# Second score pass eight slots behind the first, its rows of maxima sent by halves

## What is computed

```python
x = x + _L0_attn_ref(_layernorm(x, axis=-1), L0_attn_Wq, L0_attn_Wk, L0_attn_Wv, L0_attn_Wo)
x = x + _L0_xattn_ref(_layernorm(x, axis=-1), ctx_1024, L0_xattn_W_kv, L0_xattn_W_q, L0_xattn_W_proj, L0_xattn_b_proj)
x = x + _L0_ffn_ref(_layernorm(x, axis=-1), L0_ffn_gate_w, L0_ffn_w1, L0_ffn_b1, L0_ffn_w2, L0_ffn_b2)
```

## Time and profile before

| what | value |
|---|---|
| median of 3 runs | 202.76 us (201.15 to 203.41) |
| profiled execution | 200.95 us |
| its span, first to last instruction | 199.2 us |
| mean granted TensorE clock | 0.947 |
| TensorE busy | 166.8 us, 84% |
| VectorE busy | 140.7 us, 71% |
| ScalarE busy | 104.8 us, 53% |
| GpSimd busy | 52.3 us, 26% |

### The profile page before, as it was taken

The page is one execution under the profiler, slowest core; times in us unless marked ns, Lnnn a source line. Parts: engine busy times, 40 slices in busy tenths (PEclk is TensorE's granted clock), DMA queues, the critical chain, the costliest instruction groups (busy, mean ns, idle before and its releaser), DMA issues.

```text
span 199.2 us, 4411 instructions
## 1 busy us (share of the span) xinstructions
PE 166.8 (84%) x1500; PEld 116.1 (58%) x1508; DVE 140.7 (71%) x545; ACT 104.8 (53%) x222; POOL 52.3 (26%) x103
## 2 busy tenths in 40 slices
PE   0686195699599979989998998998998899799994
PEld 0343184485466755755764655654665556598984
DVE  2789299897347899799799889888968346525020
ACT  2132021257147656566566666766676657793451
POOL 7810005668800070030030030010115107126050
PEclk9999669589769999999999999999999999999999
DMA  5817660058227503322321321300340350170720
GB/s 150 238 35 175 164 173 18 3 148 184 70 82 196 184 25 104 110 69 58 109 82 49 98 95 35 90 0 3 113 130 3 100 143 0 17 224 26 229 66 26
DMA packets 23842, 19.05 MB, mean 96 GB/s; under 512 B 2364, under 2 KB 21820, under 8 KB 23100
## 3 DMA queue, kind: packets, MB, share of 16 engines
q1 hardware_dynamic: 22908, 17.79, 31.9%
q10 hardware_dynamic: 912, 0.98, 2.0%
HBM read 12.54 MB, written 2.49 MB: 75 GB/s over the span
## 4 chain that ended last, share of the span: by engine, by line
PE 50%; DVE 19%; DMA 15%; SPq 5%; issue 4%; POOL 3%; ACT 2%; POOLq 0%; DVEq 0%; ACTq 0%
PE psV L914 11%; PE psB L893 9%; PE psA L868 8%; DMA stackQ<-maxT 6%; DMA stackQ<-scratch 4%; DVE masked L623 4%; PE psA L958 4%; PE psM L923 3%; PE psA L975 3%; DMA stackK<-hid 3%; PE psV L975 3%; PE psM L933 3%; DVE stats L554 2%; DVE negmax L629 2%; SPq L402 2%
## 5 line engine op out<-in xcount | busy, mean ns | idle before, releaser
L753 ACT ACTIVATE E<-psB 128x512 f32<-128x512 f32 x112 | 62.3, 595 | 37.3 <-PE psB L893 15.7
L868 PE MATMUL psA<-stackK,stackQ 72*128 72x256 bf16 (+1 forms) x256 | 44.4, 277 | 11.8 <-DMA stackK<-hid 5.5
L893 PE MATMUL psB<-stackQ,stackK 74*128 74x256 bf16 (+1 forms) x256 | 42.2, 264 | 4.6 <-DMA stackQ<-maxT 3.8
L623 DVE CUSTOM_DVE_ANT_0 masked<-psA,row_mask 128x128 bf16<-128x128 f32 (+1 forms) x128 | 36.8, 352 | 11.8 <-PE psA L868 11.7
L629 DVE TENSOR_REDUCE negmax<-psA 128x2 f32<-128x512 f32 x64 | 39.7, 677 | 0.0
L868 PEld LDWEIGHTS psA<-stackK,stackQ 72*128 72x128 bf16 x256 | 23.0, 105 | 21.5 <-DMA stackQ<-scratch 8.6
L914 PE MATMUL psV<-E,V 128*9 128x256 f32 (+1 forms) x512 | 30.9, 359 | 0.2 <-ACT E L753 0.2
L893 PEld LDWEIGHTS psB<-stackQ,stackK 74*128 74x128 bf16 x256 | 22.0, 100 | 12.5 <-DMA stackQ<-maxT 5.6
L468 POOL TENSOR_SCALAR rstd<-mv 128x2 f32<-128x2 f32 x12 | 2.8, 236 | 89.1 <-DVE mv L558 88.9
L914 PEld LDWEIGHTS psV<-E,V 128*9 128x9 f32 x512 | 11.0, 90 | 14.4 <-issue 7.9
L761 ACT ACTIVATE oT<-psV 128x256 f32<-128x256 f32 x32 | 12.3, 384 | 7.9 <-PE psV L914 7.2
(11 more groups left out here) (111 smaller groups left out, 247.0 us busy)
## 6 DMA issues: line engine op xcount, KB each, us to landing
stackK<-scratch SPq DMA_DIRECT2D x18, 192.0 KB
stackQ<-hid SPq DMA_DIRECT2D x36, 64.0 KB
w1s<-w_dram SPq DMA_DIRECT2D x8, 258.0 KB, 2.8
w2s<-w_dram SPq DMA_DIRECT2D x8, 256.0 KB, 3.7
stackQ<-scratch SPq DMA_DIRECT2D x3, 576.0 KB
stackK<-hid SPq DMA_DIRECT2D x18, 64.0 KB
scratch<-hid SPq DMA_DIRECT2D x4, 192.0 KB, 3.7
scratch<-parts_ctx SPq DMA_DIRECT2D x4, 192.0 KB, 4.7
```

Of the source, the lines that this page charges most:

```text
L623: last = dve.tensor_tensor_reduce(out=masked[:, bank, i * keys:(i + 1) * keys], in0=scores[:, i, 0:keys], in1=row_mask[:, S - keys:S], sca ...
L753: act.activation(dst, psB[:, bank].rearrange("p (h q) -> p h q", h=dst.shape[1]), ACT.Exp, scale=SCALE).then_inc(b_taken, 1)
L868: last = pe.matmul(psA[:, bank, i * keys:(i + 1) * keys], stackQ[0:ROWS, b, h, t * P:(t + 1) * P], stackK[0:ROWS, b, h, 0:keys], start=Tru ...
L893: last = pe.matmul(psB[:, bank, i * n:(i + 1) * n], stackK[:, b, h, t * P:(t + 1) * P], stackQ[:, b, h, q0:S], start=(s == 1 or i == 0), s ...
```

## The change

- `LAG` is 8 instead of 11; `FFN_STEPS` puts `u0` to `u3` three slots nearer to `last`. All steps at LAG+10 and more after their job's first slot come three slots sooner; `stack_read_k` stays in its slot.
- The row of maxima goes in two halves of eight heads, each with its own transpose (`max_turn`, TensorE), copy to `maxT` and two DMAs (`max_rows`), in slots 4 and 8 after the job's first. In these slots `max_rows` stands ahead of the slot's units in the list, and `max_turn` behind them: VectorE does the copies before it takes the slot's maxima, TensorE transposes after the slot's scores. Only job 0 has both behind the units, in slot 8 also behind `rope` of batch 3. The second pass waits for the low half at group 0 and for the high half at group 2.
- Queries of cross-attention go to DRAM and back (`stack_put` at `q_cross`, `stack_get` two slots later) instead of by nine DMAs.
- `stack_write` and `stack_read` are cut into keys (1) and queries (0): batch 2's keys are written in slot 6, queries in 9, read in 9 and 10; batch 3's written in 13 and 14, read in 14 and 15 instead of 17.
- The projection of batch 3's queries and keys uses `psV` (`qk_bank`), and the memset of `psV` goes; the first `values` wait for the last rope instead. `masked` (a result that nobody reads) has two buffers instead of three.

```diff
-FFN_STEPS = ((-11, "u0"), (-10, "u1"), (-9, "u2"), (-8, "u3"), (-4, "u4"), (-3, "u5"), (-2, "u6"), (-1, "u7"),
+FFN_STEPS = ((-8, "u0"), (-7, "u1"), (-6, "u2"), (-5, "u3"), (-4, "u4"), (-3, "u5"), (-2, "u6"), (-1, "u7"),
              (1, "g0 g1"), (2, "d0 g2 d1"), (3, "d2 g3"), (4, "g4 g5 d3 d4"), (5, "s0 g6 g7 d5"), (6, "u8 d6"),
              (8, "d7 u9 d8"), (9, "s1 u10 d9 u11 d10 d11 s2"),
              (10, "u12 u13 d12 u14 d13 u15 d14 d15 s3"))
-LAG = 11
+LAG = 8
-    put(7, "max_rows", 0, 0)
...
-    put(9, "stack_write", 0, 2)
-    put(10, "stack_read", 0, 2)
-    put(14, "stack_write", 0, 3)
+    put(6, "stack_write", 0, 2, 1)
+    put(9, "stack_write", 0, 2, 0)
+    put(9, "stack_read", 0, 2, 1)
+    put(10, "stack_read", 0, 2, 0)
+    put(13, "stack_write", 0, 3, 1)
+    put(14, "stack_write", 0, 3, 0)
+    put(14, "stack_read", 0, 3, 1)
+    put(15, "stack_read", 0, 3, 0)
...
-        if j > 0:
-            put(n + 2 * NG, "max_rows", s, b)
-        if j == 1:
-            put(n + 2 * NG + 1, "stack_read", 0, 3)
+        for half in range(2):
+            if j == 0:
+                put(NG * (half + 1), "max_turn", 0, 0, half)
+                put(NG * (half + 1), "max_rows", 0, 0, half)
+            else:
+                row_of[n + NG * (half + 1)] = (s, b, half)
...
-            put(m, "stack_read_k", 1, b)
+            put(n + 21, "stack_read_k", 1, b)
             put(m + 5, "q_cross", 1, b)
-            put(m + 5, "stack_fill", 1, b)
+            put(m + 5, "stack_put", 1, b)
+            put(m + 7, "stack_get", 1, b)
...
+        if half in row_of:
+            order.append(("max_rows", *row_of[half]))
         order += [step for _, step in sorted(units, key=lambda unit: unit[0])]
+        if half in row_of:
+            order.append(("max_turn", *row_of[half]))
...
+        def qk_bank(b):
+
+            return psB[:, b % 2] if b < 3 else psV
...
-                if kind == "stack_fill" and s == 1:
-                    for i in range(NPART):
-                        for r in range(NPART):
-                            fill_q(b, i, r, parts_q[b])
-                if kind == "stack_get" and b == 1:
+                if kind == "stack_put" and s == 1:
+                    sp.wait_ge(parts_q[b], NPART)
+                    write_parts(s, b, 0, parts[:, b, 0], scr_q[b])
+                if kind == "stack_get" and s == 1:
+                    sp.wait_ge(scr_q[b], 16)
+                    read_q(s, b)
+                if kind == "stack_get" and s == 0 and b == 1:
                     sp.wait_ge(scr_q_self[b], 16)
                     read_q(s, b)
-                if kind == "stack_write" and s == 0:
-                    sp.wait_ge(parts_k_self[b], NPART)
-                    write_parts(0, b, 1, parts[:, b, 1], scr_k_self[b])
-                    sp.wait_ge(parts_q_self[b], NPART)
-                    write_parts(0, b, 0, parts[:, b, 0], scr_q_self[b])
-                if kind == "stack_read" and s == 0:
-                    sp.wait_ge(scr_k_self[b], 16)
-                    read_k(s, b)
-                    sp.wait_ge(scr_q_self[b], 16)
-                    read_q(s, b)
+                if kind == "stack_write":
+                    which = st["g"]
+                    sp.wait_ge((parts_q_self[b], parts_k_self[b])[which], NPART)
+                    write_parts(s, b, which, parts[:, b, which], (scr_q_self[b], scr_k_self[b])[which])
+                if kind == "stack_read":
+                    which = st["g"]
+                    sp.wait_ge((scr_q_self[b], scr_k_self[b])[which], 16)
+                    if which == 1:
+                        read_k(s, b)
+                    else:
+                        read_q(s, b)
...
-                    sp.wait_ge(misc_taken[st["misc"][0][0]], st["misc"][0][1])
+                    bank, k = row_use[s, b, g]
+                    sp.wait_ge(misc_taken[bank], k)
                     for i in range(2):
-                        sp.dma_start(stackQ[MAXROW + i:MAXROW + i + 1, b].rearrange("o h (t q) -> o (h t) q", t=NT),
-                                     maxT[:, b, i, :]).then_inc(maxrow_in[b], 16)
+                        heads = slice(g * NH // 2, (g + 1) * NH // 2)
+                        sp.dma_start(stackQ[MAXROW + i:MAXROW + i + 1, b, heads].rearrange("o h (t q) -> o (h t) q", t=NT),
+                                     maxT[:, b, g, i, :]).then_inc(maxrow_in[g][b], 16)
...
-                    rope_terms(psB[:, b % 2], rot[:, b % 2], rope_first)
+                    rope_terms(qk_bank(b), rot[:, b % 2], rope_first)
...
-                    bank, k = misc[0]
+                    bank, k = row_use[s, b, g]
                     dve.wait_ge(misc_full[bank], k)
                     if s == 1:
-                        dve.wait_ge(maxrow_in[b], 32)
-                    m = psM[0:NT * NH, bank, 0:P]
-                    then(dve.tensor_copy(maxT[:, b, 0, :], m))
-                    dve.tensor_tensor(maxT[:, b, 1, :], m, maxT[:, b, 0, :], ALU.subtract).then_inc(misc_taken[bank], 1)
+                        dve.wait_ge(maxrow_in[g][b], 32)
+                    m = psM[0:NT * NH // 2, bank, 0:P]
+                    then(dve.tensor_copy(maxT[:, b, g, 0, :], m))
+                    dve.tensor_tensor(maxT[:, b, g, 1, :], m, maxT[:, b, g, 0, :],
+                                      ALU.subtract).then_inc(misc_taken[bank], 1)
...
-                if kind == "max_rows":
-                    pe.wait_ge(a_taken, a_units_until(job))
-                    pe.transpose(psM[0:NT * NH, bank, 0:P], negmax[:, b], ident[:, :]).then_inc(misc_full[bank], 1)
+                if kind == "max_turn":
+                    pe.wait_ge(a_taken, a_units_until(job * NG + 2 * g + 1))
+                    heads = slice(g * NH // 2, (g + 1) * NH // 2)
+                    pe.transpose(psM[0:NT * NH // 2, bank, 0:P], negmax[:, b, heads],
+                                 ident[:, :]).then_inc(misc_full[bank], 1)
                 if kind == "scores_exp":
                     u, bank = st["u"], unit % 2
-                    if g == 0 and u == 0:
-                        pe.wait_ge(maxrow_in[b], 32 * (s + 1))
+                    if g % 2 == 0 and u == 0:
+                        pe.wait_ge(maxrow_in[g // 2][b], 32 * (s + 1))
```

More of the change, by code:

```diff
@@ L161, in plan @@
     uses = {"ln_turn": 1, "v_self": 1, "ctx_turn": 1, "k_cross": 1, "v_cross": 1, "q_cross": 1,
-            "max_rows": 1, "o_turn": 2, "o_back": 1, "o_proj": 1, "route": 1}
+            "max_turn": 1, "o_turn": 2, "o_back": 1, "o_proj": 1, "route": 1}
     count, total, steps = [0, 0], 0, []
@@ L183, in plan, with a_units_until @@
     return steps, a_unit, b_unit
-def a_units_until(job):
-    return sum(NG * GRP_UNITS[j // NB] for j in range(job + 1))
+def a_units_until(group):
+    return sum(GRP_UNITS[n // (NG * NB)] for n in range(group + 1))
 def b_units_until(group):
@@ L226, in build @@
         row_mask = sb("row_mask", [P, S])
-        masked = sb("masked", [P, NA, 2 * S], BF16)
+        masked = sb("masked", [P, 2, 2 * S], BF16)
         mask16T = sb("mask16T", [P, GH, P], BF16)
@@ L249, in build @@
         negmax = sb("negmax", [P, NB, NH, NT])
-        maxT = sb("maxT", [NT * NH, NB, 2, P], BF16)
+        maxT = sb("maxT", [NT * NH // 2, NB, 2, 2, P], BF16)
         E = sb("E", [P, 3, GH, NT, S])
@@ L619, in _ @@
                             dve.wait_ge(row_mask_set, 1)
-                        if unit >= NA:
-                            dve.wait_ge(a_taken, unit - NA + 1)
+                        if unit >= 2:
+                            dve.wait_ge(a_taken, unit - 1)
                         for i in range(nh):
-                            last = dve.tensor_tensor_reduce(out=masked[:, bank, i * keys:(i + 1) * keys], in0=scores[:, i, 0:keys],
+                            last = dve.tensor_tensor_reduce(out=masked[:, unit % 2, i * keys:(i + 1) * keys], in0=scores[:, i, 0:keys],
                                                             in1=row_mask[:, S - keys:S], scale=-1.0, scalar=LARGEST,
@@ L816, in _ @@
                     taken("ln_turn", 0, b)
-                    if b >= 2:
-                        pe.wait_ge(rope_first, b - 1)
+                    if b == 2:
+                        pe.wait_ge(rope_first, 1)
                     for w in range(2):
-                        last = pe.matmul(psB[:, b % 2, w * S:(w + 1) * S], wQK[:, w, :], xnT[:, b, :], start=True,
+                        last = pe.matmul(qk_bank(b)[:, w * S:(w + 1) * S], wQK[:, w, :], xnT[:, b, :], start=True,
                                          stop=True)
```

28 lines of the change are left out of this document (13 added, 15 removed).

## The result

The changed kernel is slower: 205.36 us in the median against 202.81 us for the kernel before on the same chip, ratio 1.021 with an interval of 1.017 to 1.025. Its profiled execution took 204.24 us with a span of 202.5 us, so +3.3 us of span against before's 199.2. The forecast was 202.6 us and no change; the time is inside the range, but no change had the highest chance (0.42), and slower by over 1%, which it is, had 0.24.

What follows compares the result with a forecast made beforehand. VectorE was taken as the bound in cross-attention. Terms of -4.2, +1.9, +0.8 and +1.35 summed to -0.15 us, span 199.0, and with 3.56 us added 202.6 us; range 198.0 to 206.0.

Steps and rivals of the forecast that it cites:

- Term 1: Second pass eight slots behind: the drain shrinks from 23.8 to 19.6 us, tail stays 28.7 us; -4.2 us.
- 0 to 3 us if it doesn't fit: Slots 8 to 15: possible cost of the three second-pass slots moved there, which were expected roughly to fit.
- Term 2: Before slot 16: batch 2's stack lands at 53.7 instead of 51.80 us, gap and low clock remain; +1.9 us.
- Term 3: Slot 20: batch 1's high row lands at 64.6 us behind batch 3's stack reads, wait 1.3 us; +0.8 us.
- the clock also falls again: Slow end of Term 3, around slot 20: the clock falls besides the wait for the row, +2.6 us.
- Term 4: VectorE, slots 16 to 63: half rows and 0.5 us transpose waits add, fewer query splits save; +1.35 us.
- The slower rival: Slots 0 and 4 mod 8: VectorE waits 1.1 instead of 0.5 us for the transpose, +4.2, total 206.8 us; chance 0.23.
- Term 5: Cross queries through DRAM: two issues instead of nine on idle SyncE, arriving before they are needed; no effect.

Runs made afterwards that it cites:

- run 5: Changed kernel with batch 3's stack read in slot 17 and batch 0's high row copied ahead of batch 3's rope: ratio 0.996 to the kernel before.
- run 9: run 5 with lag 11 and nine direct DMAs for cross queries: ratio 1.016; then also with row copies behind the slot's maxima: 0.987.
- run 6: run 5 with the context's value projections moved from slots 6, 10 and 13 to slots 35, 43 and 51: ratio 0.994.
- run 1: Changed kernel with batch 3's stack read in slot 17, behind the high row of batch 1, as before: ratio 1.000.
- run 7: run 5 with VectorE's copies of the row behind the slot's maxima instead of ahead of them: ratio 0.986, median 196.73 us.
- run 4: Changed kernel, lag 8, with cross queries sent by nine direct DMAs instead of through DRAM: ratio 1.048.
- run 9's last kernel: run 5 with lag 11, nine direct DMAs for cross queries and row copies behind the slot's maxima: ratio 0.987, median 199.0 us.

## Why the prediction was right and wrong

**Term 1, the drain: right, a little small.** -5.0 us against -4.2 from the last first-pass transpose on; the tail kept its 28.7 us. Its "0 to 3 us if it doesn't fit" was the wrong end: I put 0, and slots 8 to 15 grew by 3.2 us. Of these 1.9 us come from the high row that stands behind the rope (run 5): it holds a bank of `psM` for which the third `ctx_turn` waits, and it holds back SyncE's reads. For the 1.3 us that are left I have no single cause: the second pass fills them in run 5 (TensorE busy 16.1 of 16.5 us), but without it the stretch is as long (run 9), once by TensorE's low clock and once by the wait for batch 2's stack, whose key reads go out 5.1 us behind the start of slot 8 there, against 4.4 before. I had looked only at what VectorE and the stack would do in slots 8 to 15 and not at TensorE's own work and its clock.

**Term 2, batch 2's stack: about the right time, but not the wait.** Slot 16 started at 54.5 us (53 to 54 forecast) and the key reads at 43.4 (42.9). But TensorE did not wait for the stack and the clock did not fall behind slot 16 (1.00 in 54.5 to 62.5, 0.58 before): TensorE was as late by its own work. That the two met is luck; the stack itself was hardly sooner, since where TensorE does wait for it, it lands 10.8 us (before), 11.4 us (run 6) and 11.7 us (run 9) behind the first key read, and in the changed kernel TensorE came 11.1 us behind it. The gap of 2.31 us wasn't kept, it was filled.

**Term 3, batch 3's reads ahead of the row: the step that failed. The right mechanism, five times too small: +0.8 us forecast, some 4.2 measured.** The forecast was that the row lands behind 10 us of reads, at 64.6, and that slot 20 wants it at 63.3. It landed at 65.8, that is 10.2 us after the first read's issue, and was wanted at 62.9: everything on SyncE was 1.4 us later, because of slots 8 to 10, and slot 20 came no later since the clock was full. The wait was 2.92 us instead of 1.3. I then took 0.8 for a wait of 1.3, as if a part were slack; run 1 shows 4.2 us for 2.92. Its slots 16 to 23 say what they are made of: 1.6 us less idle time and 2.9 us less busy time for the same products, because the clock does not fall there (1.00; 0.74 in slots 20 to 23 of the changed kernel). That is the end of +2.6 us that I had kept as "the clock also falls again", and more. This is the step that turned the sign: without it the kernel is level with the one before (run 1, 1.000). The Trainium skill, "DMA: Bandwidth & Descriptors", section "Queues, rings and completion order", had two halves here: by the ring's order the row stays behind the reads, by completion that isn't first-in first-out it could land early. The row in the changed kernel, 5.6 and 6.6 us from issue to landing behind the reads, against 1.7 and 1.8 us ahead of them in run 1, agrees with the first.

**Term 4, VectorE: right in cross-attention, too small in self-attention.** 15.9 us a batch in cross-attention, the mean of three, 16.02 in the one shown (15.9 forecast), 0.45 us idle ahead of the row (0.5), none ahead of `o_proj`; slots 24 to the last transpose +1.1 us, where the sum of +1.35 was for slots 16 to 63. The slower rival put this wait at 1.1 us a place, and named 0.8 us on average as the point from which it decides. In cross-attention it was wrong. In self-attention it was right: the changed kernel has 0.97, 1.59, 4.22 and 1.13 us, run 5, where the wait at slot 20 is mended, 0.97, 1.39, 1.13 and 1.13, and the average of all ten waits is 1.07 us in the changed kernel and 0.74 in run 5. Taking the wait away is worth 1.1% at lag 8 (run 7), where slots 16 to 31 got 1.8 us shorter, and 2.9% at lag 11.

**Term 5, the way of the cross queries at nothing: right as a difference to before, wrong as a judgement.** With lag 8 it is what keeps the rows from standing 6 us behind nine issues (run 4: 1.048 against 1.021). I priced it as idle time of SyncE, which it was at lag 11 only: in run 9 TensorE has no wait for a row behind the nine issues.

**The sum.** -0.15 us of span was forecast and +3.3 measured: the drain 0.8 better, slots 8 to 15 3.2 and slots 16 to 23 4.6 longer, where terms 2 and 3 together had 2.7. That run 1 comes out at no change, as the sum had it, is luck too: there slots 8 to 15 are 3.4 us and slots 24 to 31 1.4 us longer than before, and the drain pays for it.

**What stays open.** Whether lag 8 is worth anything once the order on VectorE is mended. The ratios of run 7 and of run 9's last kernel are level (0.986 and 0.987, each to about 0.008), though the time from slot 62 to the end of the drain is 4.2 us shorter with lag 8. The profiles don't say what takes that back: slots 8 to 15 are as long (16.7 and 16.8 us), slots 16 to 31 no longer (31.3 and 31.9), slots 32 to 61 1.7 us longer with lag 8 (60.0 and 58.3), which is the one fall of the clock; and with lag 11 the profiled execution was the slowest of its six. Nor was it tried why lag 11 with rows by halves is 1.3% faster than the kernel before.

## What to carry to other kernels

A small transfer on which the next stage waits must not be issued behind large ones that nobody needs yet; its time is then theirs, and the order on the queue decides, not the moment of issue. Price a new hole on TensorE with the clock behind it: here 2.9 us of wait cost some 4.2. And where two parts of a change wait in the same stretch, test each also with the other mended: the row's order was worth 0.4% with the larger wait there and 1.1% without, and work taken out of slots 8 to 15 only uncovered the wait for the stack.
